# Scatters of 112 or 80 token rows in place of 111 or 74, in a one-core ViT layer with routed experts

## The chip, the cores and the metric

The kernel runs on one core of one Trainium2 chip, alone. The metric is the device time of one execution in microseconds (us). The core's engines have queues of their own and meet by semaphores: PE (matrix products), DVE (vector), ACT (activations), POOL (GpSimd) and SP, which issues transfers. POOL also issues the indirect transfers, whose rows go to addresses that a list in memory holds.

## What is computed

32 images of 36 patches and one class token make 32 x 37 = 1184 tokens of 256 values. The layer embeds the patches, adds a causal product attention without softmax (16 heads, rotary positions, a gate, a layer norm on its output), and then a mixture of experts, cut here to what matters:

```python
h = h + attn(layernorm(h))
x = layernorm(h).reshape(-1, 256)                  # 1184 tokens
scores = sigmoid(x @ gate_weight.T); sc = scores + gate_bias
# the two best of 4 groups (by their two best experts each), in them the 6 best of 32 experts
_, topidx = top_k(masked, 6)
tw = 0.2 * normalized(take(scores, topidx))
routed = sum over the 6: tw * (silu(x @ w_gate[e]) * (x @ w_up[e])) @ w_down[e]
lg = topidx[:, 0] // 2                             # one of 16 anchor experts, by the first choice
anchor = (silu(x @ anchor_w_gate[lg]) * (x @ anchor_w_up[lg])) @ anchor_w_down[lg]
h = h + routed + shared(x) + 0.1 * anchor
```

So each token goes to seven experts: six routed ones and one anchor.

## The kernel before

**Dense stage.** The tokens lie in eleven tiles: ten of 111 tokens (three images) and a last one of 74 (two images), `TILES = [111] * 10 + [74]`. Two tiles make a block, six blocks in all, the last with one tile. A hand-written loop over stages j runs embedding, attention and routing of neighbouring blocks against each other on PE, DVE and ACT. The normed tokens, with their 32 expert weights, a weight for the anchor and row numbers for the results, stand in `xrow`: for each tile up to 112 partitions by 322 floats (1288 bytes), one partition a token.

**Scatters.** For each block, `place` on DVE (L1233) counts for every token the rows that its seven experts' lists have reached, and L1245 writes seven row numbers a token into `slot`; semaphore `slot_ok` counts blocks. POOL waits for it and writes each tile's rows of `xrow` seven times into `rows_d` in memory, once for each choice, by the row numbers in `slot` (L457): 11 x 7 = 77 indirect transfers of 111 or 74 rows, in the order of the program. `rows_d` holds one list of rows for each of the 48 experts; SP has filled it with rows of zeros before (L378, semaphore `empty`). POOL's order at the end is written out: block 5's tiles have their anchor choice and one more scatter sent ahead of the wait for the last `slot_ok`, then come the last tile's anchor choice and the seventeen others, 18 in all. `scat_anchor` and `scat` count landed scatters. Behind them on POOL stand two memsets of a buffer for sums (L476, L480) and the sends (L483): indirect writes of 128 result rows of 1024 bytes each, 66 in all.

**List stage.** DVE works out a `table` in memory: which rows of `rows_d` each of 112 list tiles of 128 rows takes, which expert, where its weights stand. The first 25 tiles (`FIRST_ROUTED`) are anchors', the other 87 routed. SP loads the tiles in turn into six buffers (`load_rows`, L413); tile i waits for tile i - 6 to have been transposed and its columns taken, and tile 25, the first routed one, waits for all of `scat` too (L407). Tile 0 waits for `scat_anchor` and `table_ok`. For each tile PE transposes the rows (L812), ACT copies the transposed rows (L985) and the expert's weights (L981), PE makes the two products (L823), ACT the silu (L990), DVE the product of the two (L1597), PE the product back (L838), and DVE adds it weighted into a sum (L1589), having taken the tile's columns (L1566, L1574). PE's order is: tile i's products, tile i + 2's transposes, tile i - 1's product back. All engines read the tile's offsets out of `table` with register loads, all at L319. Ahead of tile 0 stand, on PE, the last shared-expert products and 4 + 8 filler matmuls (L606, L801). At the end SP loads the sums back (L419), DVE adds them to `h` and SP writes the output.

**Start.** POOL clears `ones`, `padrow`, `h` and `v_pad`, counted by `ini`, and `ring`. DVE, SP, ACT and PE wait for `ini` once each (6 of 6, or 1 on ACT's first instruction). `small` is a table of constants of 167 columns, loaded by SP (L357).

Of the kernel before, what the change touches and what calls it, by code (L numbers as in the profile page):

```python
# [24 lines left out]
P = 128  # L25
# [8 lines left out]
TP = 112  # L34
# [69 lines left out]
    return sum(copied_by_act(k) == copied_by_act(i) for k in range(i))  # L104


def number_of(i):

    return {"A": 0, "F": TILE_AXIS, "M": TILE_AXIS + FULL, "X": EXTRA_AXIS}[KINDS[i]] + INDEX[i]
# [2 lines left out]
FIRST_ROUTED = ANCHOR_TILES  # L112
EARLY_COLS = 19482
TRI4 = 3 * LISTS
SMALL = TRI4 + 23
PIECES = [[(0, 4), (4, 8), (8, NT)]] * (CHOICES - 1) + [[(0, 4), (4, 7), (7, 9), (9, 10), (10, NT)]]
assert KINDS.count("F") == FULL and KINDS.count("M") == MIXED and KINDS.count("X") == EXTRAS
assert all(KINDS[:i].count("X") >= min(EXTRAS, INDEX[i] + 1) for i in range(XT) if KINDS[i] == "M")
# [5 lines left out]
def build(nc, pt, wt, posr, brow, wqkv, wo, wg1, wg2, lnwb, gwt, gbias, sgu, sd, wx,  # L124
          ident_c, cmask_c, turn_c, parity_c, cs_c, before_c, small_c, out):
    with ExitStack() as ctx:
# [84 lines left out]
        ones = sb("ones", [P, P])  # L211
        small = sb("small", [P, SMALL])
        of_lists = small[:, 0:3 * LISTS].rearrange("p (q l) -> p q l", q=3)
        iota_a, base0, tri4 = small[:, LISTS:LISTS + ANCHORS], small[:, 2 * LISTS:3 * LISTS], small[:, TRI4:TRI4 + 16]
        pcol, number, of_number, tile_number, spare_row, last_tile, first_w = (small[:, TRI4 + 16 + q:TRI4 + 17 + q]
                                                                                  for q in range(7))
# [62 lines left out]

        B = [ctx.enter_context(nc.psum_tensor(f"B{i}", [P, 512], F32)) for i in range(8)]  # L280

        rows_d = nc.dram_tensor("rows_d", [DUMMY_ROW + 2 * P, ROW], F32).ap()
        sums_d = nc.dram_tensor("sums_d", [SPARE_ROW + P, D], F32).ap()

        ld = {n: sem(f"ld_{n}") for n in ["first", "gates", "consts", "rest", "lists", "late0", "late1"] +
# [151 lines left out]
        @block.gpsimd  # L437
        def _(pool):
            pool.memset(ones[:, :], 1.0).then_inc(ini, 1)
            pool.memset(padrow[:, :], 0.0).then_inc(ini, 1)  # L440
            pool.memset(xrow[:, :, ALPHA_COL:ALPHA_COL + 1], ANCHOR_ALPHA)
            pool.iota(token_row[:, 0, :], pattern=[[1, NT]], base=1 - NT, channel_multiplier=OWN_ROWS)
            pool.iota(token_row[:, 1, :], pattern=[[1, NT]], base=1 + TOPK * NT, channel_multiplier=OWN_ROWS).then_inc(ids_ok, 1)
            pool.wait_ge(ids_ok, 1)
            pool.tensor_copy(to_rows[:, :], token_row[:, 0, :]).then_inc(ini, 1)
            pool.tensor_copy(xrow[:, :, ROW - 1], token_row[:, 1, :]).then_inc(ini, 1)
            pool.memset(h[:, :, :], 0.0).then_inc(ini, 1)
            pool.memset(v_pad[:, :, :, :], 0.0).then_inc(ini, 1)
            pool.memset(ring[:, :], 0.0).then_inc(ring_ok, 1)
            pool.wait_ge(ini, 6)  # L450
            pool.wait_ge(empty, 32)

            def scatter(t, choices, done):

                n = TILES[t]
                for j in choices:
                    pool.indirect_dma_start(rows_d, bass.IndirectOffsetOnAxis(ap=slot[0:n, t, j:j + 1], axis=0),  # L457
                                            xrow[0:n, t, :], None).then_inc(done, 16)

            for b, tiles in enumerate(BLOCKS[:-2]):  # L460
                pool.wait_ge(slot_ok, b + 1)
                for t in tiles:
                    scatter(t, [0], scat_anchor)
                for t in tiles:
                    scatter(t, range(1, CHOICES), scat)
            pool.wait_ge(slot_ok, NB - 1)
            for t in BLOCKS[-2]:
                scatter(t, [0], scat_anchor)
            scatter(NT - 3, [1], scat)
            pool.wait_ge(slot_ok, NB)  # L470
            scatter(NT - 1, [0], scat_anchor)
            for t in range(NT - 3, NT):
                scatter(t, range(2 if t == NT - 3 else 1, CHOICES), scat)

            pool.wait_ge(hs_ok, NB)
            pool.memset(spent[:, 0:until_scattered], 0.0).then_inc(mixed_zero, 1)  # L476
            pool.wait_ge(scat_anchor, 16 * NT)
            pool.wait_ge(scat, 16 * NT * TOPK)
            pool.wait_ge(ini_d, 16 * 4)
            pool.memset(spent[:, until_scattered:MIXED * RING], 0.0).then_inc(mixed_zero, 1)  # L480

            def send(rows, src, done):
                pool.indirect_dma_start(sums_d, bass.IndirectOffsetOnAxis(ap=rows, axis=0), src, None).then_inc(done, 16)  # L483

            for t in range(ANCHOR_PACKED):
                pool.wait_ge(acc_ok, min(t + ANCHORS, ANCHOR_TILES))
                if t == ANCHOR_PACKED - 1:
                    pool.wait_ge(spared, 1)
                send(ring_rows[:, t * RING + D:(t + 1) * RING], ring[:, t * RING:t * RING + D], sent_anchor)
            for i in range(FIRST_ROUTED, XT):  # L490
                k = INDEX[i]
                if KINDS[i] == "F":
                    pool.wait_ge(Y_ok, k + 1)
                    send(tok_full[:, k:k + 1], Y[:, k, :], sent_full)
                if KINDS[i] == "M":
                    pool.wait_ge(acc_ok, sums_before(i) + 1)
                    if k == MIXED - 1:
                        pool.wait_ge(spared, 2)
                    send(mixed_rows[:, k * RING + D:(k + 1) * RING], mixed[:, k * RING:k * RING + D], sent_mixed)
# [516 lines left out]
        def _(dve):  # L1016
# [216 lines left out]
            def place(b):  # L1233

                k, t0 = len(BLOCKS[b]), BLOCKS[b][0]
                dve.wait_ge(rank_ps, b + 1)
                bank = B[1]
                step(dve.tensor_tensor(rnk[0:TT, 0:k, :], bank[0:TT, 0:k * LISTS].rearrange("p (k l) -> p k l", k=k),
                                       base[0:TT, :].unsqueeze(1).to_broadcast([TT, k, LISTS]), ALU.add))
                dve.tensor_tensor(base[:, :], base[:, :], bank[:, 2 * LISTS:3 * LISTS], ALU.add)  # L1240
                step(dve.tensor_tensor(claimed[0:TT, 0:k, :], rnk[0:TT, 0:k, :], chosen[0:TT, 0:k, :], ALU.mult))
                for u in range(k):
                    m = dve.max(top_slots[0:TT, u, :], claimed[0:TT, u, :])
                step(m)
                dve.scalar_tensor_tensor(slot[0:TT, t0:t0 + k, :], top_slots[0:TT, 0:k, :], -1.0,  # L1245
                                         ones[0:TT, 0:8 * k].rearrange("p (k e) -> p k e", k=k),
                                         ALU.add, ALU.mult).then_inc(slot_ok, 1)
                dve.wait_ge(slot_ok, b + 1)

            def embedded(b):  # L1250
# [107 lines left out]
            dve.memset(mv[:, :, :, :], 1.0)  # L1358
            step(dve.memset(nwt[:, :, :, :], 1.0))
            dve.memset(chosen[:, :, :], 0.0)  # L1360
            dve.memset(least[:, :], -BIG)
            dve.memset(unit[:, :], 1)
            dve.memset(magic[:, :, :], float(0x5F3759DF))
# [305 lines left out]
def constants():  # L1669
# [24 lines left out]
    small[:, TRI4 + 21] = last  # L1694
    small[:, TRI4 + 20] = SPARE_ROW + row
    small[:, TRI4 + 22] = [ANCHOR_COLS if i < XT and KINDS[i] != "A" else 0 for i in row]
    return dict(ident_c=np.eye(P, dtype=np.float32), cmask_c=causal, turn_c=turn, parity_c=parity, cs_c=cs.astype(np.float32),
                before_c=before, small_c=small)

# [16 lines left out]
```

## Time and profile before

| | before |
|---|---|
| runs, us | 421.48, 418.88, 420.66 (median 420.66) |
| span of the profiled execution, us | 412.1 (first to last instruction; its whole time isn't listed apart from the three runs) |
| PE busy | 343.3 us, 83% |
| DVE busy | 278.0 us, 67% |
| ACT busy | 190.0 us, 46% |
| POOL busy | 181.7 us, 44% |
| POOL, the 77 scatters (L457) | 104.1 us, 1352 ns each |
| POOL's transfer queue (q0) | 16720 packets, 19.48 MB |
| SP's transfer queue (q1) | 38192 packets, 67.66 MB |
| chain that ended last | PE 60%, DVE 20%, transfers 8%, unexplained waiting ("issue") 3%, ACT 3%, SP's queue 3%, DVE's queue 2% |

Roughly, the first 195 us of the span are the dense stage, 195 to 240 the list stage's anchor tiles, 240 to 374 its routed tiles, and the rest the sums' way back. In the list stage instructions of a line come once a tile, so the start times of one line on one engine give the pace.

### The profile page before, as it was taken

The page shows a single profiled execution, that of the slowest core. Times are in us where ns is not written, and L with a number is a line of the kernel's source. Part 1 is how long each engine was busy: PE and PEld are TensorE (multiplying, and loading weights), DVE is VectorE, ACT ScalarE, POOL GpSimd, SP SyncE. Part 2 cuts the span into 40 slices and gives each one's busy share as a digit, 9 for nine tenths or more (in the row PEclk, how much of TensorE's full clock was granted, in tenths as well). Part 3 has the DMA queues.
Part 4 walks back from the last instruction along what each step waited for, and adds up shares of the span by engine and source line. Part 5 has one row for each costly group of instructions (what it writes and reads, how often), then busy time and mean ns, then how long its engine had stood idle before and what let it go on. Part 6 is the DMA issues. An engine that isn't in the chain of part 4 may idle for free.

```text
span 412.1 us, 8817 instructions
## 1 busy us (share of the span) xinstructions
PE 343.3 (83%) x2552; PEld 299.1 (73%) x2552; DVE 278.0 (67%) x1171; ACT 190.0 (46%) x471; POOL 181.7 (44%) x159
## 2 busy tenths in 40 slices
PE   5999999999899968773889999999999999994000
PEld 3786978779687857561677789999999999993000
DVE  0466789989798886798357775555565665666675
ACT  1152153441545233400157777777877777771000
POOL 6000000588888768767871374344422344433000
PEclk9999999999999997985989999999999999998555
DMA  7999999986698643694555576555555559531998
GB/s 234 298 335 335 329 341 328 420 320 119 123 337 252 126 96 86 218 387 137 152 162 130 167 214 180 162 158 165 165 145 162 166 155 291 168 113 58 303 303 245
DMA packets 55823, 88.44 MB, mean 215 GB/s; under 512 B 16145, under 2 KB 46521, under 8 KB 55513
## 3 DMA queue, kind: packets, MB, share of 16 engines
q1 hardware_dynamic: 38192, 67.66, 52.9%
q0 software_dynamic: 16720, 19.48, 17.8%
q10 hardware_dynamic: 864, 0.73, 0.6%
q8 instruction: 21, 0.34, 0.3%
q14 instruction: 26, 0.21, 0.2%
HBM read 50.62 MB, written 37.09 MB: 213 GB/s over the span
## 4 chain that ended last, share of the span: by engine, by line
PE 60%; DVE 20%; DMA 8%; issue 3%; ACT 3%; SPq 3%; DVEq 2%; POOLq 0%
PE B L823 20%; PE B L838 10%; PE B L514 6%; PE B L812 5%; DMA W<-sums_d 4%; PE B L549 4%; PE B L632 3%; PE B L598 2%; PE B L618 2%; DVEq L319 2%; DMA e_sb<-rows_d 2%; SPq L419 2%; DVE ring L1589 1%; PE B L656 1%; DMA W<-in_pt 1%
## 5 line engine op out<-in xcount | busy, mean ns | idle before, releaser
L457 POOL DMA_INDIRECT rows_d<-spent,slot x77 | 104.1, 1352 | 97.3 <-issue 90.9
L823 PEld LDWEIGHTS B<-e_sb,UPW 128*128 128x128 f32 x796 | 105.4, 193 | 10.7 <-issue 5.5
L823 PE MATMUL B<-e_sb,UPW 128*128 128x128 f32 x796 | 108.9, 278 | 1.5 <-issue 1.5
L1597 DVE TENSOR_TENSOR e_sb<-e_sb,B 128x128 f32<-128x128 f32 (+1 forms) x112 | 32.3, 288 | 62.2 <-ACT e_sb L990 55.8
L981 ACT COPY UPW<-W 128x512 f32 (+1 forms) x112 | 63.9, 570 | 22.2 <-issue 13.9
L838 PE MATMUL B<-W,e_sb 128*128 x224 | 69.3, 391 | 0.8 <-DVE e_sb L1597 0.8
L483 POOL DMA_INDIRECT sums_d<-spent x32 | 31.1, 972 | 48.7 <-DVE spent L1589 47.9
L812 PE MATMUL B<-ident,e_sb 128*128 128x128 f32 x224 | 43.1, 274 | 1.9 <-DMA e_sb<-rows_d 1.8
L990 ACT ACTIVATE e_sb<-B 128x128 f32<-128x128 f32 (+1 forms) x112 | 30.9, 276 | 22.2 <-PE B L823 20.8
L514 PE MATMUL B<-W 128*111 128x256 f32 (+1 forms) x132 | 34.2, 406 | 4.6 <-DMA W<-in_pt 4.5
L483 POOL DMA_INDIRECT sums_d<-W,tok_full x24 | 23.2, 966 | 30.3 <-ACT W L995 29.7
L838 PEld LDWEIGHTS B<-W,e_sb 128*128 128x128 f32 x224 | 34.0, 192 | 3.5 <-issue 1.7
L985 ACT COPY e_sb<-B 128x256 f32<-128x256 f32 x88 | 32.3, 367 | 4.6 <-PE B L812 4.6
L514 PEld LDWEIGHTS B<-W 128*111 128x111 f32 (+1 forms) x132 | 23.3, 184 | 12.2 <-DMA W<-in_pt 5.3
L1589 DVE SCALAR_TENSOR_TENSOR spent<-B,wcol,spent 128x256 f32<-128x256 f32 (+1 forms) x63 | 30.4, 482 | 1.7 <-DVE spent L1574 0.8
L812 PEld LDWEIGHTS B<-ident,e_sb 128*128 128x128 f32 x224 | 28.5, 144 | 2.3 <-DMA e_sb<-rows_d 2.1
L1626 DVE TENSOR_TENSOR h<-h,W 112x1024 f32<-112x1024 f32 (+3 forms) x23 | 23.2, 1047 | 8.4 <-DMA W<-sums_d 8.4
L1289 DVE TENSOR_TENSOR e_sb<-B,spent 111x444 f32<-111x444 f32 (+1 forms) x44 | 23.6, 597 | 4.1 <-PE B L598 4.1
L1566 DVE TENSOR_TENSOR wcol<-e_sb,turn 128x1 f32<-128x1 f32 x112 | 17.2, 153 | 4.0 <-PE B L812 3.8
L598 PE MATMUL B<-W 32*111 32x222 f32 (+1 forms) x176 | 15.5, 369 | 4.8 <-ACT W L909 4.8
L549 PE MATMUL B<-W 128*128 128x222 f32 (+1 forms) x96 | 18.1, 341 | 0.6 <-ACT W L886 0.6
L606 PE MATMUL B<-spent 128*128 128x256 f32 x70 | 18.6, 414 | 0.0
(250 smaller groups left out, 524.0 us busy)
## 6 DMA issues: line engine op xcount, KB each, us to landing
e_sb<-rows_d SPq DMA_DIRECT2D x112, 161.0 KB, 2.3
rows_d<-spent SPq DMA_DIRECT2D x2, 7728.0 KB, 44.4
W<-in_wx SPq DMA_DIRECT2D x1, 6643.0 KB
W<-sums_d SPq DMA_DIRECT2D x13, 448.0 KB, 9.4
W<-in_wx SPq DMA_DIRECT2D x10, 516.5 KB, 9.5
W<-in_wx SPq DMA_DIRECT2D x1, 4576.0 KB, 18.7
W<-in_pt SPq DMA_DIRECT2D x4, 666.0 KB, 6.9
W<-sums_d SPq DMA_DIRECT2D x7, 336.0 KB, 11.1
```

What stands on the lines that cost most here:

```text
L457: pool.indirect_dma_start(rows_d, bass.IndirectOffsetOnAxis(ap=slot[0:n, t, j:j + 1], axis=0), xrow[0:n, t, :], None).then_inc(done, 16)
L483: pool.indirect_dma_start(sums_d, bass.IndirectOffsetOnAxis(ap=rows, axis=0), src, None).then_inc(done, 16)
L514: m = pe.matmul(B[0][0:TILES[t], i * D:(i + 1) * D], patch_view(b)[:, c, at:at + TILES[t]], w_patch[:, c, :], start=c == 0, stop=c == PC - 1)
L549: m = pe.matmul(B[4 + half][:, c * BT:c * BT + n], w_qkv[:, k, lo:lo + P], xnT[:, k, 0:n], start=k == 0, stop=k == KC - 1)
L812: m = pe.transpose(B[i % 2][:, k * P:(k + 1) * P], G[:, i % GB, k * P:(k + 1) * P], ident[:, :])
L823: mm = pe.matmul(B[2 + i % 2][:, m * P:(m + 1) * P], UPW[:, i % 2, at:at + P], GT[:, i % 2, k, :], start=k == 0, stop=k == KC - 1)
L838: pe.matmul(B[6 + i % 2][:, 0:D], hid[:, i % 2, :], weights, start=True, stop=True).then_inc(D_ps, 1)
L981: act.copy(UPW[:, i % 2, 0:n], W[:, bass.ds(e, size)][:, 0:n]).then_inc(upw_ok, 1)
L985: act.copy(GT[:, i % 2, :, :].rearrange("p k s -> p (k s)"), B[i % 2][:, 0:D]).then_inc(gt_by[True], 1)
L990: act.activation(S[0:n, i % 2, :], B[2 + i % 2][0:n, 0:P], ACT.Silu).then_inc(silu_ok, 1)
L1589: dve.scalar_tensor_tensor(sums, B[6 + i % 2][:, 0:D], wcol[:, i:i + 1], sums, ALU.mult, ALU.add).then_inc(acc_ok, 1)
L1597: dve.tensor_tensor(out[0:n, i % 2, :], S[0:n, i % 2, :], ups, ALU.mult).then_inc(H_ok, 1)
```

## The change

Each scatter takes its tile's count rounded up to a multiple of 16: 112 rows for 111, 80 for 74. The added partitions hold no token. Their row numbers point to a new stretch of 128 rows at the end of `rows_d`, one row for each added lane and choice (10 x 7 + 6 x 7 = 112), which nothing reads. To get them, `slot` is written as `top_slots * keep + aside`: `keep` is 1 for a token's partition and 0 beside it (one column for full tiles, one for the last), `aside` is -1 for tokens and the row number for the added lanes. Both are new columns of `small`, which grows from 167 to 257 columns. `xrow` is cleared as a whole at the start, and `top_slots` once, so that the added lanes read defined values.

```diff
+def scattered(t):
+    return -(-TILES[t] // 16) * 16
...
-SMALL = TRI4 + 23
+KEEP = TRI4 + 23
+SMALL = KEEP + 2 + 8 * NT
+TRASH_ROW = DUMMY_ROW + 2 * P
...
+        keep = small[:, KEEP:KEEP + 2]
+        aside = small[:, KEEP + 2:KEEP + 2 + 8 * NT].rearrange("p (t j) -> p t j", j=8)
...
-        rows_d = nc.dram_tensor("rows_d", [DUMMY_ROW + 2 * P, ROW], F32).ap()
+        rows_d = nc.dram_tensor("rows_d", [TRASH_ROW + P, ROW], F32).ap()
...
             pool.memset(padrow[:, :], 0.0).then_inc(ini, 1)
+            pool.memset(xrow[:, :, :], 0.0).then_inc(ids_ok, 1)
+            pool.wait_ge(ids_ok, 1)
             pool.memset(xrow[:, :, ALPHA_COL:ALPHA_COL + 1], ANCHOR_ALPHA)
...
-            pool.wait_ge(ids_ok, 1)
+            pool.wait_ge(ids_ok, 2)
...
-                n = TILES[t]
+                n = scattered(t)
                 for j in choices:
                     pool.indirect_dma_start(rows_d, bass.IndirectOffsetOnAxis(ap=slot[0:n, t, j:j + 1], axis=0),
                                             xrow[0:n, t, :], None).then_inc(done, 16)
...
-                dve.scalar_tensor_tensor(slot[0:TT, t0:t0 + k, :], top_slots[0:TT, 0:k, :], -1.0,
-                                         ones[0:TT, 0:8 * k].rearrange("p (k e) -> p k e", k=k),
-                                         ALU.add, ALU.mult).then_inc(slot_ok, 1)
+                last = 1 if b == NB - 1 else 0
+                dve.scalar_tensor_tensor(slot[0:TP, t0:t0 + k, :], top_slots[0:TP, 0:k, :], keep[0:TP, last:last + 1],
+                                         aside[0:TP, t0:t0 + k, :], ALU.mult, ALU.add).then_inc(slot_ok, 1)
...
+            dve.memset(top_slots[:, :, :], 1.0)
```

No instruction changes its place among the others. The one queue that gets a long instruction more is POOL's at the start; it read so before, from the clearing of `ones` to the scatters (`spent` holds `padrow` and `xrow`, `W` holds `v_pad`):

```order
L439 MEMSET ones 128x128
L440 MEMSET spent 128x322
L441 MEMSET spent 128x11
L442 ISA
L442 IOTA token_row 128x11
L443 IOTA token_row 128x11
L445 CAST to_rows<-token_row 128x11
L446 CAST spent<-token_row 128x11
L447 MEMSET h 128x2816
L448 MEMSET W 128x768
L449 MEMSET ring 128x2570
L457 DMA rows_d<-spent,slot 57216x322 x77
```

and so with the change:

```order
L448 MEMSET ones 128x128
L449 MEMSET spent 128x322
L450 MEMSET spent 128x3542
L452 MEMSET spent 128x11
L453 ISA
L453 IOTA token_row 128x11
L454 IOTA token_row 128x11
L456 CAST to_rows<-token_row 128x11
L457 CAST spent<-token_row 128x11
L458 MEMSET h 128x2816
L459 MEMSET W 128x768
L460 MEMSET ring 128x2570
```

The memset of 3542 elements a partition, `xrow`, stands ahead of the clearing of `h` and `v_pad`; the 77 scatters follow in their old order.

## Rows read from the trace of the kernel before

**Rows 1.** Busy time by stretch: us, PE, PEld, DVE, ACT, POOL, PEclk, DMA share, GB/s
```profile
240.00:300.00 60.00, 60.00 (x466) 57.69 (x466) 33.90 (x159) 47.22 (x118) 26.66 (x28) 1.00 0.60 173
```
**Rows 2.** Chain in order of time: start us, us, what
```profile
198.48 6.87 DMA e_sb<-rows_d
```
**Rows 3.** Timeline of POOL: start us, us, engine, line, operation [idle before <- releaser]
```profile
179.11 1.35 POOL L457 DMA_INDIRECT rows_d<-spent,slot  x1 [2.69 <-DVE slot L1245]
...
207.24 1.35 POOL L457 DMA_INDIRECT rows_d<-spent,slot  x1 [0.31 <-issue]
```
**Rows 4.** Line 413, tile loads, 196 to 214 us: issue to landing
```profile
L413 SPq DMA_DIRECT2D e_sb<-rows_d x11: 333/333/808, 196.8 to 213.0; - x11
...
DMA to landing us min/median/max: 4.1/5.2/6.2
```
**Rows 5.** Line 413, tile loads, 255 to 297 us
```profile
DMA to landing us min/median/max: 2.3/3.0/3.8
```
**Rows 6.** Timeline of PE around the first list tiles
```profile
203.14 0.41 PE L812 MATMUL B<-ident,e_sb 128*128 128x128 f32 x2
205.39 0.44 PE L812 MATMUL B<-ident,e_sb 128*128 128x128 f32 x2 [1.85 <-DMA e_sb<-rows_d]
205.67 0.61 PE L823 MATMUL B<-e_sb,UPW 128*128 128x128 f32 x4
```
**Rows 7.** Line 319, register loads, 190 to 204.5 us: count, ns min/median/max, first, last
```profile
L319 DVEq TENSOR_LOAD <-scratch x3: 694/777/1812, 201.5 to 204.4; - x3
```
**Rows 8.** Line 319, register loads, 204.5 to 209 us
```profile
L319 PEldq TENSOR_LOAD <-scratch x2: 675/1210/1745, 206.1 to 208.9; - x2
```
**Rows 9.** Line 319, register loads, 255 to 297 us
```profile
L319 DVEq TENSOR_LOAD <-scratch x38: 299/308/315, 255.0 to 296.9; - x38
```
**Rows 10.** Timeline of DVE: products of list tiles 0, 2 and 3
```profile
208.46 0.29 DVE L1597 TENSOR_TENSOR e_sb<-e_sb,B 64x128 f32<-64x128 f32 x1 [2.05 <-issue]
...
211.89 0.29 DVE L1597 TENSOR_TENSOR e_sb<-e_sb,B 64x128 f32<-64x128 f32 x1 [0.78 <-ACT e_sb L990]
...
213.17 0.29 DVE L1597 TENSOR_TENSOR e_sb<-e_sb,B 64x128 f32<-64x128 f32 x1 [0.21 <-issue]
```
**Rows 11.** Line 483, sends of 128 rows, 255 to 297 us
```profile
L483 POOL DMA_INDIRECT sums_d<-W,tok_full x19: 963/964/972, 254.4 to 296.3; - x19
...
DMA to landing us min/median/max: 2.4/2.4/3.2
```
**Rows 12.** Line 457, scatters, 197.2 to 208 us
```profile
L457 POOL DMA_INDIRECT rows_d<-spent,slot x7: 1348/1350/1354, 197.3 to 207.2; - x7
...
DMA to landing us min/median/max: 5.3/5.7/7.2
```
**Rows 13.** Transfer queues 145 to 165 us: packets, MB, share; issues with count
```profile
q0 software_dynamic: 2106, 1.81, 39.7%
...
rows_d<-spent,slot POOLq DMA_INDIRECT x12, 5.9
```
**Rows 14.** Transfer queues 255 to 297 us
```profile
q0 software_dynamic: 864, 2.36, 16.1%
```
**Rows 15.** Timeline of ACT around the first list tiles
```profile
203.58 0.37 ACT L985 COPY e_sb<-B 128x256 f32<-128x256 f32 x1 [2.65 <-PE B L812]
...
206.32 0.27 ACT L990 ACTIVATE e_sb<-B 64x128 f32<-64x128 f32 x1
```
**Rows 16.** Timeline of all engines at the start
```profile
1.88 2.44 POOL L447 MEMSET h<- 128x2816 f32 x1
...
11.88 0.43 DVE L1368 TENSOR_TENSOR W<-W 111x256 f32<-111x256 f32 x1 [10.58 <-DMA W<-in_brow]
...
17.81 23.32 SPq L378 DMA_DIRECT2D rows_d<-spent  x2
```
**Rows 17.** Page: the span; moved GB/s in 40 slices; POOL's transfer queue
```profile
span 412.1 us, 8817 instructions
...
GB/s 234 298 335 335 329 341 328 420 320 119 123 337 252 126 96 86 218 387 137 152 162 130 167 214 180 162 158 165 165 145 162 166 155 291 168 113 58 303 303 245
...
q0 software_dynamic: 16720, 19.48, 17.8%
```

More of the change, by code:

```diff
@@ L1696, in constants @@
     small[:, TRI4 + 22] = [ANCHOR_COLS if i < XT and KINDS[i] != "A" else 0 for i in row]
+    small[:, KEEP] = row < TILES[0]
+    small[:, KEEP + 1] = row < TILES[-1]
+    aside = np.full((P, NT, 8), -1, np.float32)
+    trash = TRASH_ROW
+    for t in range(NT):
+        for p in range(TILES[t], TP):
+            for j in range(CHOICES if p < scattered(t) else 0):
+                aside[p, t, j] = trash
+                trash += 1
+    assert trash <= TRASH_ROW + P
+    aside[:, :, CHOICES:] = np.where(row[:, None, None] < TILES[0], -1, 0)
+    small[:, KEEP + 2:] = aside.reshape(P, -1)
     return dict(ident_c=np.eye(P, dtype=np.float32), cmask_c=causal, turn_c=turn, parity_c=parity, cs_c=cs.astype(np.float32),
```

## Prediction

> **What bounds the kernel now.** I read first which engine is full in which stretch. From 240 us on the matrix engine is: 60.00 us busy in 60.00 us [rows 1]. What happens there is a procession of 87 tiles that nothing of this change touches, so a gain ahead of 240 us is carried to the end as it is, and a change inside POOL's scatters counts only where someone waits for them. Second, the chain that ended last: its one piece that has to do with `rows_d` is the 6.87 us from the issue of a tile load to its landing, 198.48 to 205.35 [rows 2]. Third, POOL's order in time: one scatter is 1.35 us and some 0.30 us pass ahead of the next, and the last block's 18 scatters run from 179.11 to 208.59 us [rows 3]. They therefore lie over the start of the list stage, where PE takes its first tile at 203.14 us and needs the second at once.
>
> There the scatters cost in two ways. **Loads land late:** the loads of L413 took 4.1 to 6.2 us in 196 to 214 us [rows 4], against a median of 3.0 us later [rows 5]. PE stands 1.85 us for the second tile [rows 6]. **Register loads are slow:** at L319 every engine fetches its offsets from `table`. While scatters run one takes 0.69 to 1.81 us on DVE [rows 7], and the one of PE that ended ahead of its second product 1.75 us [rows 8]. From 255 us it takes 0.31 us on DVE [rows 9]. DVE's first product (L1597) thus comes at 208.46 us, after 2.05 us idle that no engine explains; the third stands at 211.89, and only from there does the pace hold, 1.28 us a tile [rows 10].
>
> That it is the scatters, and not indirect writes as such, shows in the sends of L483. They too are indirect writes by POOL, 128 rows each and of nearly the same bytes, and they run beside the same loads: 19 of them in 255 to 297 us, with tile loads at 3.0 us and register loads at 0.31 us [rows 5, 9].
>
> **What a scatter costs, and why 112 may cost less than 111.** A send of 128 rows holds POOL 0.964 us and lands in 2.4 us [rows 11]; a scatter 1.35 us, landing in 5.7 us [rows 12]. The last six of the seven scatters in that row are tile 10's, 74 rows each, and yet the seven lie within 6 ns. A third fewer rows cost the same, so it isn't rows that POOL pays for. Packets say the like: 12 scatters put 2106 packets on POOL's queue, 175 each, for 0.15 MB each [rows 13]; 19 sends 864, 45 each, for 0.12 MB each [rows 14]. So a scatter makes four times as many packets for bytes that are a fifth more. What 111 and 74 share is the factor 37: three and two shares of 37 rows. 128 is sixteen shares of 8. If a transfer is cut into equal shares, one to an engine, up to sixteen, each present scatter puts 37 rows in line on two or three engines; 112 rows are sixteen shares of 7, and 80 sixteen of 5. I take the price of a scatter after from the sends, the nearest row: 0.96 us on POOL and 2.4 us to land. The other end is no change at all, 1.35 and 5.7 us.
>
> **The sum.** (1) POOL's pitch goes from 1.65 to 0.96 + 0.30 = 1.26 us. The start of the last 18 hangs on `slot_ok` and stays at 179.11; they end at 179.11 + 18 x 1.26 = 201.8 us in place of 208.6, and the last has landed by about 203. Of itself that is worth nothing: the SP wait for `scat` stands ahead of tile 25 of the lists, whose load waits for tile 19, some 20 paces later. (2) PE's first transposes stay at 203.14 us: PE came there without a stall, out of a fixed row of filler matmuls [rows 6]. No scatter stands ahead of that. (3) Tile 1's rows, at 3 us after an issue no later than today's 198.48, are there before PE asks: 1.85 us of waiting gone. (4) The register loads after 203 us cost 0.31 us. Now DVE sets the first product: tile 0's two small operations from 203.6 us (0.2 us each), two register loads (0.65), tile 1's operations and tile 2's loads the same again: 203.6 + 2 x (0.2 + 0.65) + about 0.2 = 205.5 us. The other branch is ready by then: copy at 203.58 (0.37), product in PE, 0.65 us from its start to the silu as at 205.67 to 206.32, silu 0.27, so 204.9 us [rows 6, 15]. So the first product moves from 208.46 to 205.5. (5) ACT's silu, register load, weight copy and row copy make the second follow by about 1.0 us; the third comes a DVE pace later, 205.5 + 1.0 + 1.28 = 207.8 us against 211.89. From there both kernels run the same steps: 4.1 us won. If the loads that DVE starts at 201.5 us, while the last scatters are still landing, remain as slow as now (the first two end near 204.1), 0.5 us of it is lost: 3.6 us.
>
> (6) What the change adds. `xrow`'s memset is 3542 elements a partition; at the rate of h's, 2.44 us for 2816, it is 3.07 us of POOL at the start. Behind it stand h's memset, which ends at 4.32, `v_pad`'s 768 elements (0.67 us at that rate), and `ini`. POOL would be through by 5.0 + 3.1 = 8.1; DVE gets past its waits at 11.88 us only, the last of them one for a DMA, and SP asks at 17.8 [rows 16]: nothing, and if that cover were gone the 3.07 us whole. `small` grows by 90 columns, 46 KB; at the slowest rate of the first slices, 234 GB/s [rows 17], 0.2 us for what is queued behind it on SP, block 1's patches. No row shows whether PE has that slack, so 0 to 0.2 us; I take 0.1. The slot instruction has the same two operands of the same shape, 112 partitions instead of 111, and the `top_slots` memset lies in DVE's 10.58 us wait: nothing. The nine added lanes' rows are 1% more bytes: nothing.
>
> Sum: 4.1 - 0.1 = 4.0 us. The profiled span is 412.1 us [rows 17], so 408.1 after. The three runs shown stand 8.6 us above the span in the median (6.8 to 9.4 us), the launch around it, which I leave as it is: 420.66 - 4.0 = **416.7 us**.
>
> **Rivals.** *Descriptors are free on POOL.* The split changes, but the 1.35 us are a fixed price per scatter. Then scatters still run to 208.6 us and register loads may stay slow; only the landing improves, 1.85 us at tile 1: 418.8. For it: the seven scatters within 6 ns. Against it: sends at 0.964. The Trainium skill, "DMA: Bandwidth & Descriptors", section "Anatomy of one DMA — SWDGE (gpsimd) path", leans that way: descriptor generation is small there, and many can be emitted before it shows. By that sentence POOL would gain nothing; the two rows speak against it.
>
> *Nothing changes.* Scatters are dear for another reason, their 1288-byte rows or their offset list, and 112 rows make as many packets. Then 420.7 us, up to 0.2 more. For it: no scatter of another row count with factor 16 is in the trace. Against it: the equal times of 74 and 111 rows. The same page, section "Why a DMA increments its semaphore by 16 and not by 1", gives one rule for either rival: the engines used are the largest number up to 16 that divides the rows, but with an exception by which some POOL copies use all 16 whatever the rows. By its rule the spread comes; by its exception 111 rows would be spread already and this rival holds. The equal POOL times of 74 and 111 rows, 1.35 us, side with the rule.
>
> *Slower.* Now every scatter has a share on every engine. A load needs all sixteen, and today it meets fewer: 5.7 us of landing over 1.65 us of pitch is 3.5 scatters in flight, some ten engines' shares. If meeting a share is what delays a load, sixteen in place of ten make tile 1's 6.87 us 11.0: 4.1 us lost, 424.8. It decides as soon as that landing exceeds 6.87. Against it: the sends meet the loads on their engines too, if they are spread, and the loads took 3.0 us.
>
> **How the numbers follow.** The forecast gets 0.68, with a range of its own of 415.3 to 417.7 (the two bounds of step 4, the 0.2 us of step 6 and the runs' spread); free descriptors 0.12; nothing 0.13; slower 0.07. The range 414.9 to 419.6 leaves out the last two. A measurement of this kernel tells about 1% from no change, 4.2 us here: below 416.45 lies somewhat less than half of the forecast's case, 0.31; above 424.9 about half of the slower case and nothing else, 0.04; the rest 0.65.
>
> **What would show it.** Right: POOL's scatters at 0.95 to 0.97 us, the last ending near 202; POOL's queue far below its 16720 packets [rows 17] (77 x some 130 fewer, near 6,700); tile loads from 196 us on at 3 us; register loads after 203 us at 0.3; PE's 1.85 us wait gone, the first product near 205.5, the third near 207.8, the third's lead intact at the last list tile. Wrong: scatters at 1.35 us (a rival above); a third product that comes late although the loads are there (step 4 missed a wait); or a lead that has gone by 240 us (what bounds the list stage was not DVE).

## The result and the profile after

The changed kernel takes 414.99 us in the median of its runs (411.44 to 418.71), the kernel before, timed beside it, 419.06 us (415.61 to 425.43). The ratio is 0.9907, with a 95% interval of 0.9881 to 0.9933: 3.9 us faster, of which the interval leaves 2.8 to 5.0. Some runs of each kernel are some per cent longer than its others; the ratios leave them out, and `clear_only` and `no_clear` below were profiled in such runs. The forecast was 416.7 us, and 4.0 us of gain.

The page of after, the lines that answer to [rows 17] and to the table of before:

```profile
span 413.0 us, 8819 instructions
...
q0 software_dynamic: 6864, 19.48, 14.0%
...
L468 POOL DMA_INDIRECT rows_d<-spent,slot x77 | 73.8, 959 | 121.7 <-DMA rows_d<-spent 68.9
```

The 77 scatters (L457 before, L468 now) hold POOL 73.8 us in place of 104.1, and its queue has 6864 packets in place of 16720 for the same 19.48 MB. The span, though, is 413.0 us where before's profile had 412.1. The profiled execution of after took 414.79 us in all, so 1.8 us lie around a span. By that the profiled execution of before took some 413.9 us, well below the median of its runs; absolute times of the two traces can't be compared, and what follows compares stretches between two events of one trace.

POOL's last block after, the answer to [rows 3] (start, duration, idle time before it and what ended that):

```profile
183.88 0.91 POOL L468 DMA_INDIRECT rows_d<-spent,slot  x1 [4.35 <-DVE slot L1257]
...
204.91 0.91 POOL L468 DMA_INDIRECT rows_d<-spent,slot  x1 [0.30 <-DMA rows_d<-spent,slot]
```

Eighteen scatters pass in 21.9 us; before, they took 29.5. The transfer queues in 150 to 169 us answer to [rows 13]:

```profile
q0 software_dynamic: 624, 1.88, 32.2%
...
rows_d<-spent,slot POOLq DMA_INDIRECT x14, 2.7
```

A scatter lands in 2.7 us, not 5.9, and puts 48 packets on the queue (13 of these 14 fall in the stretch), not 175. At the start of the list stage the timelines of PE and DVE, the tile loads (L422) and DVE's register loads (L328) answer to [rows 4, 6, 7, 10]:

```profile
205.45 0.60 PE L823 MATMUL B<-ident,e_sb 128*128 128x128 f32 x4
```
```profile
DMA to landing us min/median/max: 2.3/2.8/3.4
```
```profile
L328 DVEq TENSOR_LOAD <-scratch x38: 298/308/421, 206.2 to 229.6; - x38
```
```profile
208.03 0.29 DVE L1609 TENSOR_TENSOR e_sb<-e_sb,B 64x128 f32<-64x128 f32 x1 [0.49 <-issue]
209.07 0.29 DVE L1609 TENSOR_TENSOR e_sb<-e_sb,B 64x128 f32<-64x128 f32 x1 [0.49 <-issue]
210.32 0.29 DVE L1609 TENSOR_TENSOR e_sb<-e_sb,B 64x128 f32<-64x128 f32 x1 [0.19 <-issue]
```

PE takes tiles 0 and 1 in one go, with no bracket and so no wait; loads land in 2.8 us in the median; a register load takes 0.31 us from the first tile on. The third product comes 4.87 us after the first transposes; before, it came 8.75 us after.

Stretches of this kind from eight traces, each read from the timelines of DVE and PE (us). "Slots" is the last write of `slot`, "table product" PE's first product of the table (L711 before, L722 after), "transposes" the first of the lists:

| kernel | scatter rows | slots at | slots to table product | to transposes | to third product | sum of the three |
|---|---|---|---|---|---|---|
| before | 111/74 | 178.6 | 13.96 | 10.55 | 8.75 | 33.3 |
| before, again | 111/74 | 178.4 | 13.74 | 10.37 | 10.17 | 34.3 |
| `additions` | 111/74 | 181.6 | 14.02 | 11.65 | 8.65 | 34.3 |
| `clear_only` | 111/74 | 183.1 | 13.80 | 11.05 | 8.99 | 33.8 |
| `no_clear` | 111/74 | 184.8 | 13.87 | 10.76 | 7.47 | 32.1 |
| after | 112/80 | 183.4 | 12.63 | 9.44 | 4.87 | 26.9 |
| after, again | 112/80 | 181.6 | 12.66 | 10.03 | 4.76 | 27.5 |
| `rows117` | 117/78 | 181.7 | 12.74 | 10.06 | 5.02 | 27.8 |

The mean of the five with dear scatters (1.35 us on POOL) is 33.6 us (34.0 without `clear_only` and `no_clear`), of the three with cheap ones (0.94 to 0.99 us) 27.4. The 6.2 us between them have three parts: 3.9 at the third product, 1.2 ahead of the table product, 1.0 between. The first two repeat from trace to trace. The third isn't shown to come from the rounding: after's two traces differ by 0.6 us in it, and `paced` below, with cheap scatters too, has 10.66. From the third product to the last one it is 162.6 us in before and in after, so the lead reaches the end.

### The profile page after: what moved, and what is told of

Its sections match the earlier page's. It is cut to its first block, busy times and chain, and to the rows that moved or that the text cites. A ratio compares the mean times of both kernels' runs of the same rounds, so it can differ in the third digit from the quotient of the medians.

```text
span 413.0 us, 8819 instructions
## 1 busy us (share of the span) xinstructions
PE 344.4 (83%) x2552; PEld 298.7 (72%) x2552; DVE 277.3 (67%) x1172; ACT 189.7 (46%) x471; POOL 154.6 (37%) x160
## 3 DMA queue, kind: packets, MB, share of 16 engines
q0 software_dynamic: 6864, 19.48, 14.0%
## 4 chain that ended last, share of the span: by engine, by line
PE 60%; DVE 19%; DMA 7%; issue 4%; ACT 3%; DVEq 3%; SPq 3%; POOLq 0%
PE B L834 19%; PE B L849 10%; PE B L525 5%; DMA W<-sums_d 5%; PE B L823 5%; PE B L560 4%; PE B L643 3%; PE B L609 2%; PE B L714 2%; DVEq L328 2%; DMA W<-in_wg 2%; PE B L629 2%; SPq L428 2%; DVE ring L1601 1%; PE B L667 1%
## 5 line engine op out<-in xcount | busy, mean ns | idle before, releaser
L468 POOL DMA_INDIRECT rows_d<-spent,slot x77 | 73.8, 959 | 121.7 <-DMA rows_d<-spent 68.9
L1001 ACT ACTIVATE e_sb<-B 128x128 f32<-128x128 f32 (+1 forms) x112 | 30.9, 276 | 21.9 <-PE B L834 19.6
```

The source lines that it names most:

```text
L1001: act.activation(S[0:n, i % 2, :], B[2 + i % 2][0:n, 0:P], ACT.Silu).then_inc(silu_ok, 1)
```

## The experiments

**The two kernels again.** The first row of each pair was one trace; these are second ones.

> The kernel before once more, for a second profile. Its first profile had no stretch in 76 to 140 us in which PE ran at the lower clock, and reached the list's first transposes at 203.14 us; the five profiles that hold the additions (with the rounding and without) each had one or two such stretches in 83 to 140 us, 1.2 to 1.6 us each, and got the sixth block's slots 2.8 to 4.8 us later. Theory C: the first profile of before was a quick execution of it, and this one has such a stretch too, first transposes at 205 to 207 us. Theory B: before has none, and the additions bring them; first transposes at 203 us again. The list start, first transposes to third product, is 8 to 9.5 us by both.

> The changed kernel once more, for a second profile. In its first profile the dense stage reached PE's first transposes of the list stage 2.3 us later than the kernel before did (205.45 against 203.14 us), while from there to DVE's third product it took 4.87 us against 8.75. Theory A: the later start is this one execution's; in this profile the first transposes stand near 202 us or earlier (203.14 less about 1.2 us that the table's vector instructions gained), the 4.87 us come again to 0.3 us, and the ratio is 0.985 to 0.995. Theory B: the change itself delays the dense stage by 2 to 4 us; then the first transposes stand near 205 us again.

Before took 415.58 us in its one run, after 415.15 in the median of ten, with a ratio of 0.9933 (0.9897 to 0.9969). The stretches above repeat: third product 10.17 and 4.76 us after the transposes. In this trace of before POOL stood 8.45 us between two scatters near 130 us, and the last one came 35.0 us after the slots, not 28.6; its third product is the latest of all, although PE took tiles 0 and 1 in one go: DVE's register loads (L319, 199 to 214 us) took 1.04 us in the median.

The first transposes stand at 202.55 us in before and at 204.26 in after. By the forecasts both are nearer to theory B, a delay by the change itself; but both traces of before, some 413.9 and 415.58 us, lie below its median of 419.06, so this doesn't decide.

**The additions without the rounding.** After, with the row count of before:

```
-    return -(-TILES[t] // 16) * 16
+    return TILES[t]
```

> The changed kernel with the rounding alone undone: 111 and 74 rows again, with the larger constant table, the clearing of xrow and the new slot instruction left in. Prediction's step 6 and theory A: these are worth 0 to 0.2 us, ratio 0.998 to 1.003, scatters at 1.35 us, first transposes to third product 8 to 9.5 us. Theory B: they delay the dense stage, 2 to 4 us more than the kernel before, ratio 1.005 to 1.010.

The ratio to before is 1.0056 (1.0017 to 1.0095): the additions cost 0.7 to 4.0 us, in the middle 2.3. At the list start everything is as before: the first transposes wait for their rows, and DVE's register loads (L328, 199 to 214 us) are slow.

```profile
207.27 0.82 PE L823 MATMUL B<-ident,e_sb 128*128 128x128 f32 x4 [1.13 <-DMA e_sb<-rows_d]
```
```profile
L328 DVEq TENSOR_LOAD <-scratch x8: 565/906/2144, 204.5 to 212.8; - x8
```

So the row count alone, not the way `slot` is made, brings the gain at the list start. What the rounding is worth by itself follows from the two ratios: 0.9907 / 1.0056 = 0.985, some 6.2 us, which is what the table of stretches gives; with after's second ratio, 0.9933, timed beside `additions`, it is 0.988, some 5.1 us.

**Which addition costs.** `clear_only` is before with the clearing of `xrow` alone; `no_clear` is `additions` without it.

```
+            pool.memset(xrow[:, :, :], 0.0).then_inc(ids_ok, 1)
+            pool.wait_ge(ids_ok, 1)
```

> The kernel before with one of the additions alone: the clearing of xrow on POOL at the start (3.07 us). The additions together, without the rounding, cost 0.56% [0.17%, 0.95%], some 2.3 us. Theory A (the clearing carries the cost: it keeps POOL and what waits for it later): ratio 1.004 to 1.007, the last block's row numbers (slot) at 181 us or later. Theory B (the clearing is hidden at the start, as the prediction said, and the cost is that of the larger table of constants and the new slot instruction): ratio 0.998 to 1.002, row numbers at 178.3 to 178.8 us as in both profiles of before.

> The additions without the clearing of xrow: table of constants of 257 columns in place of 167, slot made with keep and aside, top_slots cleared, rows_d longer; scatters stay 111 and 74 rows. Theory A (clearing): ratio 0.998 to 1.002, row numbers of the last block at 178.3 to 178.8 us. Theory B (the rest): ratio 1.004 to 1.007, row numbers at 181 us or later. If both kernels lose half or neither loses, the delay isn't one part's but a property of the dense stage that small shifts set off.

`clear_only` has a ratio of 1.0030 (0.9989 to 1.0070), `no_clear` 1.0048 (1.0012 to 1.0084). The second interval leaves out a loss of zero, the first does not, but the two overlap too far to be told apart. Neither theory fits as it stood: theory A (the clearing carries all) has `no_clear`'s loss against it, theory B `clear_only`'s slots at 183.1 us, where it wanted 178.3 to 178.8. That both kernels lose a part, the third case of `no_clear`'s forecast, fits as well, so which addition costs stays open. The traces give one small thing that goes with the new table and slot instruction. DVE, at the same instruction, in `clear_only` and in `no_clear`:

```profile
33.29 2.20 DVE L1291 TENSOR_TENSOR e_sb<-B,spent 111x444 f32<-111x444 f32 x4 [0.16 <-PE B L600]
```
```profile
34.20 2.20 DVE L1298 TENSOR_TENSOR e_sb<-B,spent 111x444 f32<-111x444 f32 x4 [0.57 <-PE B L607]
```

The idle time ahead is 0.16 us in both traces of before and in `clear_only`, 0.57 us in after and `no_clear`. A second such place is on PE near 80 us:

```profile
80.75 1.02 PE L600 MATMUL B<-W 32*111 32x222 f32 x16 [0.81 <-ACT W L911]
```
```profile
81.98 1.02 PE L607 MATMUL B<-W 32*111 32x222 f32 x16 [1.12 <-ACT W L918]
```

Together 0.4 + 0.3 = 0.7 us, of an instruction that waits longer although its operand comes from the same place; why, the rows don't say. A further part shows as the granted clock. Windows of 100 to 125 us (PE, PEld, DVE, ACT, POOL busy, PEclk, DMA share, GB/s), of after and of `additions`:

```profile
100.00:125.00 25.00, 23.64 (x204) 19.28 (x203) 21.30 (x95) 10.05 (x21) 13.81 (x14) 1.00 0.64 222
```
```profile
100.00:125.00 25.00, 23.45 (x195) 18.70 (x194) 19.83 (x91) 9.27 (x17) 20.68 (x15) 0.93 0.72 217
```

In a stretch of 0.93 matmuls run in part at the lower of the two clocks, and the block of 24.8 us takes 26.5 in `additions` (slots 98.3 to 124.8). In the two traces of before no window between 78 and 150 us is below 1.00; in after 78 to 100 and 125 to 150 are, 0.92 and 0.93. After's second trace has none there (the forecast of `before_again` counted it among the five that have), but 0.62 from 160 to 170 us, where before has 0.84 and 0.85, and the block there takes 25.7 us (slots 148.0 to 173.8) in place of 24.3 and 24.2. Each of the twelve other traces has at least one block 1.2 us or more longer than before's; `clear_only`, with neither the larger table nor the new slot instruction, has two (26.5 and 25.8). So the place of these stretches changes from execution to execution, and whether the additions make them likelier stays open: both traces of before lie below its median, so that their slots at 178.5 are no fair mark for the 181 to 185 of the others.

**Scatters in flight, or POOL's end?** The list start could be late because dear scatters run beside it, or because POOL ends late. `full112` and `last80` round only one kind of tile; `paced` has 112/80 rows, with a small memset after each scatter that brings the pitch near 1.5 us.

```
-    return -(-TILES[t] // 16) * 16
+    return TILES[t] if t == NT - 1 else 112      # full112
+    return 80 if t == NT - 1 else TILES[t]       # last80
...
+                    pool.memset(idle[:, :], 0.0).then_inc(idle_ok, 1)      # paced
+                    pool.wait_ge(idle_ok, idles[0])
```

> The changed kernel with 112 rows for the ten full tiles, 74 for the last. Now twelve scatters behind the last slots are cheap and the last six dear: POOL ends near 11 x 1.25 + 7 x 1.65 = 25.3 us after them, earlier than with the last tile alone rounded, but the six dear ones run over the first transposes. Theory D: the register loads there are slow as before, the third product follows by 7 to 8.5 us, more than in the kernel with 80 rows for the last tile. Theory E: less than there.

> The changed kernel with 80 rows for the last tile, 111 for the ten others. Of the 18 scatters behind the last slots the first twelve are then dear (11 of 111 rows and one of 80), the last six cheap: POOL ends near 12 x 1.65 + 6 x 1.25 = 27 us after them, later than with 112 rows in the full tiles alone, but from some 5 us ahead of the first transposes only cheap ones start. Theory D (what costs is dear scatters in flight): register loads after the first transposes take 0.3 us, the third product follows them by 4.9 to 5.6 us. Theory E (what counts is when POOL is through): it ends at or after the first transposes, the third product follows by 7 us or more. The table's vector instructions keep their stalls (slots to table 13.7 us) by both.

> The changed kernel with a small memset of an unused buffer behind each scatter, which POOL waits for, so that the pitch is 1.6 to 1.75 us as with 111 rows and the last scatter starts some 29 us after the last slots, over the first list tiles. Theory D: cheap scatters in flight hurt neither loads nor register loads, so first transposes to third product stay at 4.9 to 5.6 us. Theory E: the list start falls back to 7 us or more. The slots-to-table time stays near 12.4 us if POOL's stalls of DVE come from the writing of many descriptors, and goes back to 13.7 if from POOL being busy at all.

One run each (417.15, 419.21 and 416.97 us). The last scatter of POOL, the first transposes and the third product, first of `full112`, then of `paced`:

```profile
205.16 1.35 POOL L468 DMA_INDIRECT rows_d<-spent,slot  x1 [0.30 <-DMA rows_d<-spent,slot]
```
```profile
205.01 0.60 PE L823 MATMUL B<-ident,e_sb 128*128 128x128 f32 x4
```
```profile
211.07 0.29 DVE L1609 TENSOR_TENSOR e_sb<-e_sb,B 64x128 f32<-64x128 f32 x1 [0.19 <-issue]
```
```profile
208.67 0.92 POOL L470 DMA_INDIRECT rows_d<-spent,slot  x1 [0.28 <-POOL idle L472]
```
```profile
206.02 0.60 PE L828 MATMUL B<-ident,e_sb 128*128 128x128 f32 x4
```
```profile
211.00 0.29 DVE L1614 TENSOR_TENSOR e_sb<-e_sb,B 64x128 f32<-64x128 f32 x1 [0.19 <-issue]
```

`paced` goes on scattering 2.7 us past its first transposes and still has the third product 4.98 us after them. `full112` issues its last, a dear one, with the transposes, and needs 6.06, less than the 7 to 8.5 that theory D gave it. `last80`, whose last ones are cheap and run 2 us past the transposes, needs 5.23. In these traces, one for each, what the lists meet in flight decides, not when POOL is through; theory D has the order right and the size of `full112` wrong. The dear ones that are left in `full112` cost 1.2 us, against 3.9 where they run on for another 4 us, as in before. The table product comes 13.1 to 13.4 us after the slots in all three, between the two groups of the table; for `paced` it is 13.2, between the 12.4 and the 13.7 of its forecast, so the question put there stays open.

**Other row counts.** Is 16 the point, or equal shares? 117 is thirteen shares of 9, 78 thirteen of 6; 113 and 79 are primes.

```
-    return -(-TILES[t] // 16) * 16
+    return 78 if t == NT - 1 else 117      # rows117
+    return 79 if t == NT - 1 else 113      # rows113
```

> Scatters of 117 and 78 rows, 13 times 9 and 13 times 6, no multiple of 16. Theory of equal shares (a transfer is cut into the largest number of equal parts up to 16, 13 here; POOL's price goes by the rows of a part): POOL 0.97 to 0.99 us, landing about 2.7 us, first list transposes to third product 4.9 to 5.2 us, span 411 to 414 us. Rival (only multiples of 16 are cheap): 1.35 us on POOL, transposes to third product 8 us or more, span 415 to 419 us.

> Scatters of 113 and 79 rows, two primes: two rows more than before, and no equal cut but into single rows or one part. Theory of equal shares: one part of 113 rows. From 8 rows a part at 0.964 us and 37 at 1.35 us POOL's price rises 0.0133 us a row, so 0.96 + 105 x 0.0133 = 2.36 us, pitch 2.66 us; 59 scatters from 78 us take until 235 us, the row numbers of the last tile wait for none of them, all 77 end near 283 us, and the first routed tile waits for them: span about 460 us. Rival (rows or bytes are what counts): 0.95 to 1.35 us on POOL, span 411 to 419 us.

The page of `rows117`, then of `rows113`:

```profile
q0 software_dynamic: 7984, 19.92, 14.5%
...
L468 POOL DMA_INDIRECT rows_d<-spent,slot x77 | 77.5, 1006 | 117.1 <-DMA rows_d<-spent 67.0
```
```profile
span 573.4 us, 8819 instructions
...
q0 software_dynamic: 39120, 20.07, 15.0%
...
L468 POOL DMA_INDIRECT rows_d<-spent,slot x77 | 180.2, 2340 | 196.1 <-issue 195.8
```

`rows117` does as forecast: 0.99 us on POOL, third product 5.02 us after the transposes, 413.57 us. `rows113`, two rows more than before, takes 575.25 us. Its price on POOL was forecast to the hundredth, 2.36 us, but not its whole time: I had 460 us. POOL stands idle besides: of the 195.8 us that no engine explains 67.7 lie ahead of the first scatter, as 68.9 do in before, and 128.1 between scatters, 1.7 us each in place of 0.3:

```profile
289.56 2.36 POOL L468 DMA_INDIRECT rows_d<-spent,slot  x1 [0.30 <-issue]
302.32 2.36 POOL L468 DMA_INDIRECT rows_d<-spent,slot  x1 [10.40 <-issue]
304.99 2.37 POOL L468 DMA_INDIRECT rows_d<-spent,slot  x1 [0.30 <-issue]
```

A few scatters follow each other at 2.66 us, then one stands 10.4. That looks like a queue that has filled and must drain, which would also explain the 8.45 us in before's second trace; it was not tested. The first list tile waits 132.6 us for its rows:

```profile
337.94 0.66 PE L823 MATMUL B<-ident,e_sb 128*128 128x128 f32 x2 [132.64 <-DMA e_sb<-rows_d]
```

**Fillers.** With the third product early, the filler products ahead of the first transposes may be too many. `nofill` drops the eight of L801 (L812 after), `lessfill` also three of the four ahead of them at L606.

```
-            for _ in range(8):
-                pe.matmul(B[3][:, 0:P], ident[:, :], ident[:, :], start=True, stop=True)
...
-            stay_busy(4, 3, w_sgu)
+            stay_busy(1, 3, w_sgu)      # lessfill
```

> The changed kernel without the 8 filler matmuls (1.95 us) that stand on PE ahead of the list's first transposes; nothing reads their results. By prediction's step 2 the filler alone holds PE now, since the loads have landed by then. Theory A: the transposes move up by up to 1.95 us, DVE, which adds the last shared rows about 0.6 us after the transposes could start, lets the third product follow 1.2 to 1.6 us earlier, total 413.5, ratio to before about 0.987. Rival: the filler keeps the granted clock up, and without it PE runs the first tiles at half the clock and nothing is won (0.990 or above).

> As the kernel without the 8 fillers, and of the four 128x256 fillers ahead of the last shared product three are gone too (1.4 us). Theory A: PE reaches the transposes up to 3.3 us earlier than with the change alone; the loads of tile 0 and 1, issued near 199.8 and 200.5 us at 2.3 to 3.4 us, are there just in time; third product 2 to 3 us earlier, ratio to before about 0.983 to 0.985. Rival: the loads or the clock bind now, no more than without the 8 fillers, 0.987 to 0.990.

The ratios to before are 0.9879 (0.9835 to 0.9923) and 0.9870 (0.9831 to 0.9909), beside 0.9933 (0.9897 to 0.9969) of after in the same comparison. Both are faster than before and their middles lie below after's, but the intervals overlap, and `lessfill` stays above its 0.983 to 0.985. In the traces the stretch from the table product to the third product shrinks from 14.8 us (after, again; 14.3 in after's first trace) to 13.8 and 13.7. Beside after, again, the transposes come 1.8 to 2.1 us earlier after the table product, and the third product gets back only some 1 us of it, because its stretch grows to 5.6 and 5.8 us.

## Why the prediction was right, and where it was not

**What bounds it** was read rightly: the lead of the third product stands at the last one (162.6 us between them in both traces).

**Step 1, POOL's pitch.** Forecast 1.26 us, measured 1.24 (0.94 + 0.30) for 112 rows, 1.21 for 80. The queue has 6864 packets; "near 6,700" was said, as a send was put at 45 packets and has 48.

**Step 2, the first transposes stay.** Wrong in size, and in the good direction. From the slots to the transposes it was 24.5 us and is 22.1. I had followed the register loads and the tile loads, which the scatters slow, and not DVE, which works out the table while POOL scatters. The same four instructions, of before and of after (lines 12 further down):

```profile
179.75 0.69 DVE L1447 CAST e_sb<-whole 128x32 f32<-128x32 int32 x1
...
181.35 0.74 DVE L1454 TENSOR_SCALAR e_sb<-e_sb 128x32 f32<-128x32 f32 x1
...
183.12 0.63 DVE L1466 CAST e_sb<-whole 128x16 f32<-128x16 int32 x1
...
186.32 0.73 DVE L1488 TENSOR_SCALAR e_sb<-e_sb 128x32 f32<-128x32 f32 x1
```
```profile
184.56 0.21 DVE L1459 CAST e_sb<-whole 128x32 f32<-128x32 int32 x1
...
185.68 0.34 DVE L1466 TENSOR_SCALAR e_sb<-e_sb 128x32 f32<-128x32 f32 x1
...
187.10 0.18 DVE L1478 CAST e_sb<-whole 128x16 f32<-128x16 int32 x1
...
189.86 0.17 DVE L1500 TENSOR_SCALAR e_sb<-e_sb 128x32 f32<-128x32 f32 x1
```

In before they are 1.9 us longer together, and the table product comes 1.3 us earlier in after. Each of the four of before ends within 0.03 us of the end of a scatter, the first of that at 179.11 us [rows 3], the others of these:

```profile
180.76 1.35 POOL L457 DMA_INDIRECT rows_d<-spent,slot  x1 [0.30 <-issue]
182.42 1.35 POOL L457 DMA_INDIRECT rows_d<-spent,slot  x1 [0.30 <-issue]
185.73 1.35 POOL L457 DMA_INDIRECT rows_d<-spent,slot  x1 [0.30 <-issue]
```

The Trainium skill, "SBUF — State Buffer", section "SBUF: two separate sides", has a pair of ports that DVE (in some of its operations) and GpSimd share under an exclusive lock, where the later one stands still until the other is through. Rows of 0.17 to 0.34 us that become 0.63 to 0.74 and end with the scatter agree with that, though no run here took DVE off those ports. The rest, about 1 us, is PE's. In before it stood 8.31 us ahead of the table product, in after 6.98, and in after it comes back to the higher of its two clocks sooner. That the scatters do this is not shown: `rows117` stood 8.77 us and needs 10.06 us from there to the transposes, `paced` with its cheap scatters 7.55 and 10.66, before 10.55. The pair of products behind the table product takes 1.06 and 0.59 us, at a granted clock of 0.50 (1.2 GHz) and of 1.00 (2.4 GHz); timeline and window of before, then of after:

```profile
192.59 1.87 PE L711 MATMUL B<-ident,tcol 128*1 128x128 f32 x8 [8.31 <-DVE tcol L1524]
...
196.23 1.06 PE L717 MATMUL B<-e_sb,ones 128*128 128x256 f32 x2
```
```profile
196.20:197.20 1.00, 1.00 (x4) 0.79 (x3) 0.00 (x0) 0.00 (x0) 0.80 (x1) 0.50 0.34 82
```
```profile
196.01 1.87 PE L722 MATMUL B<-ident,tcol 128*1 128x128 f32 x8 [6.98 <-DVE tcol L1536]
...
199.34 0.59 PE L728 MATMUL B<-e_sb,ones 128*128 128x256 f32 x2
```
```profile
199.30:199.90 0.60, 0.60 (x5) 0.52 (x5) 0.19 (x1) 0.00 (x0) 0.43 (x1) 1.00 0.39 129
```

**Steps 3 and 4** came as worked out: PE's wait of 1.85 us is gone, register loads are at 0.31 us, and the first product comes 2.58 us after the transposes (2.36 forecast). The wait of step 3 isn't in every execution, though: before's second trace has none for tile 1 and still has its third product 10.17 us after the transposes, with 1.99 and 2.52 us of DVE idle that no engine explains. What repeats is the slow register loads of step 4.

**Step 5**, the third product 4.66 us after the transposes: 4.87, 4.76 and 5.02. Of the 4.1 us that it was to bring, 3.9 came.

**Step 6, the additions for 0.1 us**, is the term that failed: 2.3 us (0.7 to 4.0). That the clearing's 3.07 us are hidden, as said, isn't shown: `clear_only`'s 1.0030 is 1.3 us, with an interval of -0.5 to 2.9. The larger table and the new slot instruction, put down at 0.1 and at nothing, carry a loss that excludes zero (`no_clear`, 2.0 us, 0.5 to 3.5). Two stalls of 0.7 us in sum go with them; the rest isn't explained. The added lanes are sixteen, not nine, 1.4% more rows.

**The sum** of 4.0 us against 3.9 measured is thus partly luck: some 2.2 us of gain missed at step 2, of which 1.0 may be chance, stand against some 2.2 of loss missed at step 6. Nor do 8.6 us of launch lie around the span; it is 1.8, and the profile was of an execution below the median. As the sum was a difference taken from the median, that did no harm.

**The rivals.** That descriptors cost POOL nothing falls with 1.35 us becoming 0.94, and rising to 2.36 in `rows113`. That nothing changes falls with the packets, that loads meet more shares and get slower with their 2.8 us. Of the rule and the exception in the Trainium skill, "DMA: Bandwidth & Descriptors", section "Why a DMA increments its semaphore by 16 and not by 1", these scatters follow the rule: 117 rows go as 13 shares, 113 as one (the sizes of packets at the end show it).

## What to carry to other kernels

Give an indirect write a row count that divides into many equal shares, and never a prime; dummy rows that pad it are cheap beside what they save. Look at the packets of POOL's queue before its bytes: they tell what a write costs POOL and everyone who works beside it. And price helper edits (a larger constant table, a clearing, another operand) by a run of their own, as here they took in the middle more than a third of what the rounding gained.

## What the runs showed of the hardware

**Packets by the rows of one share.** With r rows in a share, every scatter and send of these runs fits 16 x (r/4, rounded up, + 1) packets, however many of the sixteen shares carry rows. Before: 77 x 176 + 66 sends x 48 = 16720; after: 143 x 48 = 6864; `rows117`: 70 x 64 + 73 x 48 = 7984; `rows113`: 70 x 480 + 7 x 336 + 66 x 48 = 39120. All four are the page's numbers to the packet, and so are 7760 of `full112` and 15824 of `last80`. The sizes of the packets in the traces show the shares. A full packet holds four rows (5152 bytes of a scatter, 4096 of a send), and what is left of a share goes in a smaller one. In before 224 packets hold one row (1288 bytes): one for each of the 70 x 3 + 7 x 2 shares of 37 rows. In `rows117` 910 do, 70 x 13; in `rows113` 70, one for each scatter of 113. The rest, 12368 packets of 4 or 16 bytes in before and 2288 of 4 in after, carry no row, so an engine without rows of its own still gets as many packets as the fullest one.

**POOL's price by packets.** 48 packets 0.94 us, 64 0.99, 176 1.35, 336 1.91, 480 2.36: about 0.79 us + 3.3 ns a packet.

**Who pays beside POOL.** While scatters of 176 packets run, register loads take 0.6 to 2.1 us in place of 0.31, and some short operations on DVE, which then end with a scatter, 0.6 to 0.7 in place of 0.2 to 0.3.
